# A four-layer gated decoder on one core: attention rebuilt with stacked queries and keys, scores formed twice, and value products that keep the values stationary

## What is computed

```python
x = x + tanh(g_xattn[l]) * xattn_l(layernorm(x), ctx, ctx, mask_l)   # 16 heads of depth 8, 77 keys
x = x + tanh(g_ffn[l])   * ffn_l(layernorm(x))
```

```python
s = einsum('qhd,khd->hqk', q, k) * scale + mask   # 512 x 77 for each of 16 heads
out = einsum('hqk,khd->qhd', softmax(s), v) @ Wo
```

## Time and profile before

| | us |
|---|---|
| three runs | 969.97, 961.72, 963.01 |
| median | 963.01 |
| span of the profiled execution (first to last instruction) | 960.8 |
| its mean granted TensorE clock | 0.893 of 2.4 GHz |
| PE busy | 767.5 (80%) |
| DVE busy | 664.4 (69%) |
| ACT busy | 301.0 (31%) |
| POOL busy | 236.8 (25%) |

### The profile page before, as it was taken

The page is one execution under the profiler, slowest core; times in us unless marked ns, Lnnn a source line. Parts: engine busy times, 40 slices in busy tenths (PEclk is TensorE's granted clock), DMA queues, the critical chain, the costliest instruction groups (busy, mean ns, idle before and its releaser), DMA issues.

```text
span 960.8 us, 13366 instructions
## 1 busy us (share of the span) xinstructions
PE 767.5 (80%) x4914; PEld 592.3 (62%) x4914; DVE 664.4 (69%) x1496; ACT 301.0 (31%) x548; POOL 236.8 (25%) x539
## 2 busy tenths in 40 slices
PE   3685787456559999986898991289998899999998
PEld 2474666344447777764677771167777677777775
DVE  3967987698875576649777774956665766757554
ACT  2242343221214433432333540135344322222211
POOL 3633421244550141137334322401211000000000
PEclk9697998676779999999799995579999799999999
DMA  6650000000000000001010000000001000000000
GB/s 139 36 76 1 1 1 1 0 1 0 1 0 1 1 1 1 1 1 62 1 50 2 1 1 1 0 1 1 1 1 51 1 1 1 12 1 12 1 12 12
DMA packets 51195, 11.68 MB, mean 12 GB/s; under 512 B 44108, under 2 KB 50316, under 8 KB 50748
## 3 DMA queue, kind: packets, MB, share of 16 engines
q1 hardware_dynamic: 51132, 10.84, 6.1%
HBM read 9.16 MB, written 1.68 MB: 11 GB/s over the span
## 4 chain that ended last, share of the span: by engine, by line
PE 58%; DVE 28%; issue 6%; ACT 4%; POOL 2%; DMA 1%; SPq 0%; DVEq 0%
PE ps L1099 14%; PE ps L1281 8%; PE ps L1064 6%; PE ps L1072 5%; PE ps L1086 4%; DVE xn L670 4%; PE ps L1259 3%; PE ps L1261 3%; PE ps L1260 3%; DVE mx L702 3%; ACT pt L473 3%; DVE pq L705 3%; PE ps L1270 2%; PE ps L1115 1%; DVE st L656 1%
## 5 line engine op out<-in xcount | busy, mean ns | idle before, releaser
L1099 PE MATMUL ps<-vb,pt 128*128 128x144 f32 x1280 | 175.4, 294 | 11.5 <-DVE loT L692 9.6
L1099 PEld LDWEIGHTS ps<-vb,pt 128*128 128x128 f32 x1280 | 167.5, 197 | 14.3 <-issue 14.1
L473 ACT ACTIVATE pt<-ps 128x512 f32<-128x512 f32 (+1 forms) x192 | 94.1, 524 | 145.3 <-PE ps L1086 142.9
L702 DVE TENSOR_REDUCE mx<-ps 128x8 f32<-128x616 f32 x128 | 101.5, 793 | 20.7 <-PE ps L1072 19.0
L496 ACT ACTIVATE pq<-pq 128x616 f32<-128x616 f32 x128 | 88.1, 712 | 82.6 <-DVE pq L705 82.3
L1086 PE MATMUL ps<-ident,pq 128*128 128x128 f32 x640 | 99.1, 290 | 15.2 <-ACT pt L473 15.2
L705 DVE TENSOR_TENSOR pq<-ps,mx 128x616 f32<-128x616 f32 x128 | 102.3, 800 | 4.4
L713 DVE RECIPROCAL rd<-ps 128x16 f32<-128x16 f32 x64 | 16.4, 256 | 116.6 <-PE ps L1099 116.5
L1086 PEld LDWEIGHTS ps<-ident,pq 128*128 128x128 f32 x640 | 74.8, 147 | 33.4 <-ACT pt L473 30.3
L955 DVE TENSOR_TENSOR pq<-ps,pq 128x512 f32<-128x512 f32 x72 | 49.8, 691 | 64.2 <-ACT pq L566 57.0
L381 POOL TENSOR_TENSOR nt<-nhv,rs 128x4 f32<-128x4 f32 x108 | 24.4, 226 | 279.5 <-DVE rs L663 273.4
(11 more groups left out here) (223 smaller groups left out, 1298.3 us busy)
## 6 DMA issues: line engine op xcount, KB each, us to landing
mst<-in_moe_gate SPq DMA_DIRECT2D x1, 1152.0 KB, 4.9
mst<-in_moe_up SPq DMA_DIRECT2D x1, 1152.0 KB, 5.0
pt<-in_moe_down SPq DMA_DIRECT2D x1, 1152.0 KB, 5.1
x<-in_x SPq DMA_DIRECT2D x4, 256.0 KB, 6.1
out<-x SPq DMA_DIRECT2D x4, 256.0 KB, 2.3
wp<-in_wp SPq DMA_DIRECT2D x1, 704.0 KB, 4.0
v_bounce<-vs SPq DMA_DIRECT2D x4, 154.0 KB
m1f<-in_m SPq DMA_DIRECT2D x1, 616.0 KB, 5.1
```

Source lines behind the costliest of these rows:

```text
L473: act.activation(pt[:, t % 2, 4 * r:4 * r + w, :], ps[:, 4 + R % 2, 0:w * P].rearrange("p (c q) -> p c q", q=P), ACT.Copy).then_inc(evac_d ...
L702: link(dve.tensor_reduce(m, sc, AX_X, ALU.max))
L1099: ins = pe.matmul(ps[:, 6, 0:VW], pt[:, t % 2, c, :], vb[:, n % 2, c, :, :].rearrange("p h e -> p (h e)"), start=c == 0, stop=c == NC - 1)
```

## The change

The attention of all four layers is replaced; the feed-forward parts keep their instructions (layer 3's inputs and buffers get names of their own). There are now 16 batches `n = 4 l + b` instead of 64 tiles.

- **Stacked operands.** `QG` holds for each group 106 rows: q high, q high again, q low (32 rows each), two rows for masks, eight rows of maxima. `KG` holds k high, k low, k high, two mask rows, and eight rows of -1 where a column belongs to the head. They are filled by transfers inside SBUF: 12 for q, 12 for k, 4 for the maxima, and 6 that place v in `VN`, for every batch, each with three buffers. GpSimd makes `kmH` and `kmL` (`key_rows`) as it made `kH` and `kL`; `vb`, `vc` and the way through DRAM go.
- **Scores by token** (`scores`): 16 products for a batch, 98 rows x 308 columns, only for the maxima. VectorE takes a maximum of 308 columns for each (`maximum`), in two PSUM banks taken in turn. GpSimd splits the maxima in two parts, TensorE turns them in one transposition, ScalarE copies, SP puts them into `QG`.
- **Scores by key** (`turned_scores`): 12 products for a batch (4 groups x 3 chunks of 110, 88 and 110 keys) with KG stationary and QG moving, 106 rows x 512 columns; the rows of maxima subtract them. ScalarE takes the exponential from PSUM to SBUF (12 for a batch). No transposition of probabilities is left, nor their copy, nor the subtraction on VectorE.
- **Value products** (`weighted_sum`): 12 fp32 products for a batch, with 36 columns of `VN` stationary (4 heads x 8 values and 4 columns of ones) and 512 tokens moving. Neighbouring groups write at partition 0 and at partition 64 of one bank. Two are issued after every second score product, four after the last. The sums are copied out, turned in 8 transpositions, divided, turned again in 4, and projected.
- **Masks**: layer 1 adds two reduced-fp32 passes to every product of both kinds, layer 2 one bf16 pass, layer 3 none (its mask is in the mask rows).
- **Order**: a loop over `k` from -2 to 4 with 12 slots each; in stage `k` TensorE forms the turned scores and sums of batch `k`, the scores by token of `k+1`, q of `k+2`, and ends batch `k-1`. SP issues 604 transfers instead of 62.

```diff
+CH = [(0, 110), (110, 88), (198, 110)]
+KS, KZ = 98, 106
+LAG = 2
@@ sync
+            def keys(n):
+                if n >= 3:
+                    sp.wait_ge(st_ps, NCH * (n - 2))
+                sp.wait_ge(km_ready, n + 1)
+                for g in range(G):
+                    r = slice(32 * g, 32 * g + 32)
+                    sp.dma_start(KG[0:32, n % 3, g, :].bitcast(F32), kmH[r, n % 2, :].bitcast(F32)).then_inc(kg_in[n % 3], 16)
...
+            def queries_in(n):
+                sp.wait_ge(q_hi, n + 1)
+                sp.wait_ge(q_lo, n + 1)
...
+            def maxima_in(n):
+                sp.wait_ge(mT_ready, n + 1)
+                for g in range(G):
+                    sp.dma_start(QG[98:106, n % 3, g, :].bitcast(F32), mT[32 * g:32 * g + 32, n % 2, :].bitcast(F32)).then_inc(mg_in[n % 3], 16)
...
+            for l in range(L):
...
+                for k in range(-2, B):
+                    if k + 2 < B:
+                        queries_in(l * B + k + 2)
...
+                    if 0 <= k + 1 < B:
+                        maxima_in(l * B + k + 1)
...
+                    if k >= 0 and l * B + k + 3 < N:
+                        keys(l * B + k + 3)
+                        values(l * B + k + 3)
@@ scalar
+                for k in range(-2, B + 1):
+                    for c in range(NCH):
+                        if 0 <= k < B:
+                            weigh(k, c)
+                        if c == 0 and k + 2 < B:
+                            xT_one(k + 2)
+                        if c == (3 if k >= 0 else 1) and k + 2 < B:
+                            q_one(k + 2)
+                        if c == 10 and 0 <= k + 1 < B:
+                            maxima_out(k + 1)
...
@@ vector
+                if l == 2:
+                    weight8_magnitude()
+                    inner_norm_residual(3)
+                for k in range(-2, B + 1):
+                    for c in range(NCH):
+                        if c == (3 if k >= 0 else 0) and k + 2 < B:
+                            q_rest(k + 2)
...
+                        if c < 8 and 0 <= k + 1 < B:
+                            for u in (2 * c, 2 * c + 1):
+                                maximum(k + 1, u // G, u % G)
+                        if c in (3, 5) and k >= 1:
+                            normalise(k - 1, (c - 3) // 2)
...
@@ tensor
+                def scores(b, i, g):
...
+                    if u >= 2:
+                        pe.wait_ge(max_done, u - 1)
+                    o = ps[:, u % 2, 0:GK]
+                    ins = pe.matmul(o, QG[0:KS, n % 3, g, q], KG[0:KS, n % 3, g, :], start=True, stop=l not in (1, 2))
...
+                def turned_scores(b, c):
...
+                    if c == 0:
+                        pe.wait_ge(mg_in[n % 3], 64 * uses(n))
+                    if q >= 2:
+                        pe.wait_ge(exp_done, q - 1)
+                    o, r = ps[0:w, 4 + q % 2, :], slice(r0, r0 + w)
+                    ins = pe.matmul(o, KG[0:KZ, n % 3, g, r], QG[0:KZ, n % 3, g, :], start=True, stop=l not in (1, 2))
...
+                def weighted_sum(b, c):
...
+                    p0 = 64 * (g % 2)
+                    pe.matmul(ps[p0:p0 + VC, 6 + g // 2, :], VN[0:w, n % 3, g * 3 + j, :], PT[0:w, q % 4, :],
+                              start=j == 0, stop=j == 2, skip_group_check=True).then_inc(pv_done, 1)
...
+                for k in range(-2, B + 1):
+                    for c in range(NCH):
+                        if c == 0 and k + 2 < B:
+                            turn_input(k + 2)
+                        if c == (3 if k >= 0 else 0) and k + 2 < B:
+                            queries(k + 2)
+                        if c < 8 and 0 <= k + 1 < B:
+                            for u in (2 * c, 2 * c + 1):
+                                scores(k + 1, u // G, u % G)
+                        if 0 <= k < B:
+                            turned_scores(k, c)
+                            if c >= LAG and c % 2 == 1:
+                                weighted_sum(k, c - LAG - 1)
+                                weighted_sum(k, c - LAG)
...
+                        if c == 10 and 0 <= k + 1 < B:
+                            turn_maxima(k + 1)
+                    if 0 <= k < B:
+                        for c in range(NCH - LAG, NCH):
+                            weighted_sum(k, c)
```

More of the change, by code:

```diff
@@ L72, in program @@
         xnT = sb("xnT", [P, B, S])
-        hiT = sb("hiT", [P, B, S], F32R)
-        loT = sb("loT", [P, B, S], F32R)
         ident = sb("ident", [P, P])
@@ new lines, in _ @@
+            sp.dma_start(wp[:, 3:11, :], a["wp"][:, 3:11, :]).then_inc(ld_w2, 16)
+            sp.dma_start(l2rep[:, :, :], a["l2rep"]).then_inc(ld_w2, 16)
+            sp.dma_start(bq[:, :], a["bq"]).then_inc(ld_w2, 16)
+            sp.dma_start(rows[:, :, :], a["rows"].partition_broadcast(P)).then_inc(ld_w2, 16)
+            sp.dma_start(gates[:, :], a["gates"].partition_broadcast(P)).then_inc(ld_w2, 16)
+            for r in range(3):
+                sp.dma_start(VN[:, r, :, :], a["vn"]).then_inc(vn_zero, 16)
@@ L279, in _ @@
+            for n in range(2):
+                keys(n)
+                values(n)
+            next_mask(0)
+            keys(2)
+            values(2)
+            sp.dma_start(m3f[:, :, :], a["m3"].partition_broadcast(P)).then_inc(ld_const, 16)
+            sp.dma_start(repb[:, :], a["repb"]).then_inc(ld_const, 16)
             sp.dma_start(w1s[:, :], a["w1"]).then_inc(ld_ffn1, 16)
@@ new lines, in q_rest, with maximum @@
+                    dve.wait_ge(q_hi, n + 1)
+                    if n >= 2:
+                        dve.wait_ge(qg_in[(n - 2) % 3], 192 * uses(n - 2))
+                    dve.scalar_tensor_tensor(out=loT[:, n % 2, :], in0=ps[:, 2, :], scalar=bq[:, l:l + 1],
+                                             in1=hiT[:, n % 2, :].bitcast(F32), op0=ALU.add,
+                                             op1=ALU.subtract).then_inc(q_lo, 1)
+                def maximum(b, i, g):
+                    n = l * B + b
+                    u = n * 4 * TPB + i * G + g
+                    dve.wait_ge(s_ps, u + 1)
+                    if i == 0 and g == 0 and n >= 2:
+                        dve.wait_ge(m_split, n - 1)
+                    dve.tensor_reduce(mraw[:, n % 2, i, g * HG:(g + 1) * HG],
+                                      ps[:, u % 2, 0:GK].rearrange("p (h k) -> p h k", k=K), AX_X, ALU.max).then_inc(max_done, 1)
@@ L1111, in project, with att_transposed @@
+                def att_transposed(b):
+                    n = l * B + b
+                    pe.wait_ge(att_done, 2 * n + 2)
+                    for i in range(TPB):
+                        ins = pe.transpose(ps[:, 3, i * P:(i + 1) * P], att[:, i, :], ident[:, :])
+                    ins.then_inc(attT_ps, 1)
                 def project(b):
@@ L1313, in layout @@
     r = np.arange(P)
-    flat = np.arange(NC * P)
-    owner = np.where(flat < HK, flat // K, -1)
-    e = np.arange(NE)
+    owner = np.arange(GK) // K
+    turned = np.arange(GK) % K
+    vn = np.zeros((110, NCH, VC), f)
+    for h, k0, k1, j, r0 in RUNS:
+        for g in range(G):
+            vn[r0:r0 + k1 - k0, g * 3 + j, HG * DH + h] = 1
     a = dict(
```

785 lines of the change are left out of this document (414 added, 371 removed).

## The result

| | us |
|---|---|
| kernel before, runs beside it | 966.49 median (961.72 to 971.08) |
| changed kernel, four runs | 1034.87 median (1027.56 to 1051.63) |
| ratio | 1.068, 95% interval 1.060 to 1.076 |
| forecast | 944, range 908 to 992 |

The prediction was wrong, outside its range. The profiled execution of the changed kernel is its longest run (1051.6 us, span 1049.8, mean granted clock 0.744), and the ratio leaves it out, as every ratio here leaves out runs over 1.5% above the fastest of their kernel, while medians are of all runs. The three others have clocks of 0.753 to 0.769, the kernel before 0.893. So the profiled stages are read for what happens in them, and the sizes of effects come from the medians.

What follows compares the result with a forecast made beforehand. TensorE was taken as the bound, VectorE for much of attention 0. Layers 0 to 3 gave -16.4, +5.4, -2.8, -13.5, sum -27.3; with +8 for the clock, 960.8 became 941.5, 944 us as median; range 908 to 992.

Steps and rivals of the forecast that it cites:

- TensorE's clock, +8 us (0 to 24): Whole program: clock restarts at half after idle; two idle stretches a layer, 1 us each, +8 us, between 0 and 24.
- Wait (a): Slot 3 of a stage: VectorE's `q_rest` waits for ScalarE and delays the next maxima; about 1.4 us lost.
- Wait (c): Stage's end: maxima reach QG about 5 us after the last maximum, TensorE has some 3.4 left; 0.9 us lost.
- Value products, 7.4 us: Middle stage: 12 products, neighbours on two halves partly overlapped, 7.4 us, between 5.2 ideally paired and 10.5 serial.
- Rival B: Value products: both halves run fully together, 7.4 becomes 5.2 us a stage; total 917 us; chance 0.14.
- Rival A: Value products run one after the other, +2.9 to 3.1 us a stage; total 985 us, slower; chance 0.27.
- Stages, 18.4, 21, 21 and 21.7 with the tail: Each layer's four batches without mask passes: first 18.4, middle two 21 each, last 14.5 plus 7.2 after it; 82.1 us.
- SP, "16.2 us, below 21: nothing": SP's queue: 34 issues a batch take 16.2 us, less than a middle stage of 21, so they cost nothing.
- Rival C: Transfers cost more: 0.6 us an issue, 20.4 a batch, landings at 2.8; +18 to +25, total 965; chance 0.15.
- The head, first scores at 59.8: Program start, layer 0: 98 issues ahead of q's, then 12 for q and a landing, put first scores at 59.8 us.
- The way in, 20 us: Each layer, q to first turned score: issues 5.7, landing 2, 16 scores 7.2, the maxima's way 5.0; 20 us.
- Layer 1, +5.4: Attention of layer 1: two mask passes for each product make it end later, 418.1 against 414.0, with feed-forward's wait +5.4 us.

Runs made afterwards that it cites:

- e17: e15 without the 14 added matmuls ahead of a layer's first scores, and 22 instead of 30 ahead of its first turned score; 950.36 us, ratio 0.983.
- e13: e10 with VectorE's `q_rest` in slot 5 instead of slot 3 (the edit of e12); 963.95 us, ratio 0.998.
- e10: Changed kernel with e2, e3 (14 for 40 matmuls before first scores), each layer's first q on two queues, scored group by group; 992.50 us.
- e3: Changed kernel plus unread matmuls in TensorE's waits: 40 before a layer's first scores, 30 before its first turned score, 20 before each later stage's; 1016.65 us.
- e4: Changed kernel with all value products written to the first half of the output partitions (output not the reference's); 1024.41 us, ratio 1.061.
- e11: e3 with the edit of e4, all value products on the first half (output not the reference's); 1045.05 us, ratio 1.081.
- e15: e13 with the edit of e1, key transfers of batches 3 to 15 issued by ScalarE, one a slot; 956.33 us, ratio 0.991.
- e1: Changed kernel with the 12 key transfers of every later batch issued by ScalarE instead of SP, one a slot; 1069.45 us.
- e8: e3 without the key transfers of batches 3 to 15 (output not the reference's); 1027.18 us.
- e2: Changed kernel with SP's order in layer 0 changed: q of batch 0 ahead of values and later keys; 1029.84 us, ratio 1.056.
- e12: Changed kernel with VectorE's `q_rest` in slot 5 instead of slot 3 in stages 0 and 1 of each layer; 1016.35 us, ratio 1.053.

## Why the prediction was wrong, by its own steps

1. **TensorE's clock, +8 us (0 to 24): the step that failed.** It was priced as two restarts a layer, each over when work is back. But the clock falls also inside stages, behind waits of 1.4 us and more, and then stays at half for 14 to 27 us, nearly all of it full work. In attention 3 the four stages took 94.5 us; with the clock held up (e17's 77.0, its 3 x 2.8 us of added matmuls taken off) 68.6. Of the 25.9 between them 8.3 are three waits for SP's transfers (3.37 and 2.35 shown above, 2.61 at 810.74) and 2.5 the two waits behind `q_rest`; the rest, an estimate, is about 15 us in one layer, nearly twice what I gave all four.
2. **Wait (a), 1.4 us behind `q_rest`: right in place and size (1.45), wrong in price.** It was priced by its length, 11 us in sum for the eight, and taking them down was worth 28.5 us (e13 against e10). In the traces of the change, e3 and e10 there are 24 such waits of 0.88 to 1.46 us: 18 were followed by a fall within 2.5 us, 6 by none for 13 us or more. In e4 and e11 they are 0.60 or less, and no fall followed any of them for 18 us. Wait (c), for the maxima, was too small too: 0.9 in the sum, 1.4 to 2.9 in the trace (2.35 at 786.80).
3. **Value products, 7.4 us: too dear.** Rival B was right on the mechanism: both halves run together. A pair starts 0.99 us ahead of what follows it at full clock, and six are 5.9:

```profile
127.44 1.05 PE L1227 MATMUL ps<-PT,VN 88*36 88x512 f32 x4
128.43 0.49 PE L1207 MATMUL ps<-QG,KG 106*110 106x512 f32 x1
```

The Trainium skill, "TensorEngine Tiling (Array Packing)", Theoretical Speedup, gives up to twice the speed for 64 columns or fewer, and the trace agrees: 1.91 for a pair on one half, 1.06 on two. Rival A's mechanism is refuted; that its time, 985, was the nearest of all is luck.

4. **Stages, 18.4, 21, 21 and 21.7 with the tail: too dear as well.** e17 has 15.5, 18.2, 15.4 and 19.4 without the added matmuls. Part of the difference is that e17 no longer has waits (a) and (c), 2.3 us of a middle stage of 21. Both errors of TensorE's own work were on the dear side, so they hid some of the loss.
5. **SP, "16.2 us, below 21: nothing": wrong.** It is 24.8. Rival C had the price (0.6 an issue, 20.4 a batch) and took it for a hitch. It shows while the clock is up: the second stage of attention 3 went from 23.85 us (e13) to 20.66 with the keys on another queue (e15), and e1 and e8, where the clock in it was 0.86, gained nothing. The Trainium skill, "DMA: Bandwidth & Descriptors", Rules for kernel authors, says to join many small transfers, as under 64 KB one pays mostly overhead; that pointed the right way, but no run here joined any.
6. **The head, first scores at 59.8: 73.3.** The same price: the 98 issues took 63.6 us where 52.1 was forecast, 0.63 or 0.88 each for those inside SBUF, and q's own 12 took 7.6 for 5.7. The sum carried the head in full to the end of attention 0; of the 25 us that e2 took away 15 were left there, so part of it was covered.
7. **The way in, 20 us: 24.7** in attention 3 (711.91, just after q's low half is ready, to 736.63): issues 7.6 for 5.7, scores at half clock 9.6 for 7.2 (eight pairs, one every 1.2).
8. **Layer 1, +5.4: +42.** Its first two stages in the changed kernel, then in e17:

```profile
334.22:376.53 42.31, 40.86 (x115) 24.45 (x116) 8.93 (x20) 9.57 (x17) 5.36 (x8) 0.55 0.11 27
376.53:413.96 37.43, 34.58 (x134) 22.16 (x132) 13.56 (x37) 10.17 (x18) 5.79 (x17) 0.73 0.15 34
```

```profile
305.30:331.43 26.13, 26.13 (x138) 17.47 (x136) 9.31 (x21) 9.58 (x17) 5.37 (x8) 1.00 0.17 40
331.43:359.44 28.01, 27.91 (x153) 19.04 (x152) 12.83 (x35) 10.40 (x18) 6.34 (x17) 1.00 0.22 50
```

Without the added matmuls e17's are 23.3 and 25.2, 7.8 and 7.0 above those of attention 3, where 7.8 was forecast for the masks: their passes were priced nearly rightly, and most of the 31 us between the two kernels here is the clock.

That pairs end sooner and so lengthen the wait from 0.60 to 1.45 is what the two timelines show. Whether something else in pairs lowers the clock stays open: e12 kept the pairs and took that wait away, and its mean clock rose by 0.01 where e4, with the wait at 0.60 and no pairs, rose by 0.07. Part of it can be read from the traces: serial products also shorten the waits for the maxima's transfer, 17.9 us in sum in e4, 30.3 in e12 and 27.5 in the change, and before the attentions' tails e4's clock falls only twice, behind waits of 1.58 and 2.07, where e12's falls nine times. No run isolates this. Why e1's runs are spread so widely (clocks of 0.72 to 0.76) stays open too.

## What to carry to other kernels

When a change makes TensorE's work denser in bursts and adds waits between them, price each wait by what the granted clock does behind it, from a stretch of the trace where it fell and one where it did not, not by the wait's length; and look for a cheap move that fills or removes the wait before judging the change. Price every transfer by an issue of its own kind, and compare the queue's sum with the stage at full clock. An edit tested alone on a kernel with another bound can hide its worth: the keys' move won nothing alone and 8 us once the clock was held.
